# Self-attention's values with transposed probabilities as the weights, queries in the partitions

## The reference

```python
x = x + cross_attention(layernorm(x), ctx_1024)      # softmax(q ctx^T) ctx, one head
x = x + self_attention(layernorm(x), w_attn, w_proj)
x = x + moe_ffn(layernorm(x), Wg, W1, W2, W3)        # 8 experts, each takes its 32 best tokens

def self_attention(x, w_attn, w_proj):               # T = 256, 16 heads of 16
    q, k, v = split(x @ w_attn.T)                    # each (16, T, 16)
    att = einsum('bhqd,bhkd->bhqk', q, k) / sqrt(16)
    att = att + where(rel <= 0, slope[h] * rel, -inf)   # causal, rel = key - query
    y = einsum('bhqk,bhkd->bhqd', softmax(att), v)
    return y.reshape(T, 256) @ w_proj.T
```

## Time and profile before

| | us |
|---|---|
| median of 3 runs | 124.24 |
| lowest and highest | 122.81, 124.9 |
| the profiled execution | 122.81 |
| its span, first to last instruction | 121.1 |
| TensorE busy (matmuls), share | 108.1, 89% |
| VectorE busy, share | 77.5, 64% |
| ScalarE busy, share | 60.3, 50% |

### The profile page before, as it was taken

How to read it: one execution, slowest core, us unless ns; L and a number is a source line. 1 busy time by engine, 2 the same in 40 slices (tenths; PEclk the granted TensorE clock), 3 DMA queues, 4 the chain that set the end, 5 groups by cost and what they waited for, 6 DMA issues and landing times.

```text
span 121.1 us, 2466 instructions
## 1 busy us (share of the span) xinstructions
PE 108.1 (89%) x958; PEld 89.0 (73%) x958; DVE 77.5 (64%) x194; ACT 60.3 (50%) x114; POOL 50.6 (42%) x65
## 2 busy tenths in 40 slices
PE   4999999999999999999998959892987995899981
PEld 4968888888999999999978648681955794334540
DVE  0699889977659697357339799979044797021212
ACT  4377779549869657541248894870011302514100
POOL 2499999999999999911010000010001400300000
PEclk9999999999999999999999999999599999999999
DMA  2995999995999400006989898000000000000002
GB/s 98 375 405 166 401 355 353 419 424 219 346 433 433 179 5 0 0 5 173 520 346 520 346 514 346 11 8 0 5 0 0 0 0 0 5 0 0 0 5 87
DMA packets 3756, 22.72 MB, mean 188 GB/s; under 512 B 544, under 2 KB 800, under 8 KB 3232
## 3 DMA queue, kind: packets, MB, share of 16 engines
q1 hardware_dynamic: 3744, 22.55, 47.1%
HBM read 22.29 MB, written 0.26 MB: 186 GB/s over the span
## 4 chain that ended last, share of the span: by engine, by line
PE 78%; DVE 15%; issue 3%; ACT 1%; POOL 1%; POOLq 0%
PE bank L842 6%; PE bank L844 6%; PE bank L843 6%; PE bank L816 6%; PE bank L820 6%; PE bank L823 6%; PE bank L935 6%; PE bank L1028 6%; PE bank L832 6%; PE bank L798 3%; PE bank L904 3%; PE bank L1043 3%; PE bank L882 3%; DVE att_T L562 3%; PE bank L916 2%
## 5 line engine op out<-in xcount | busy, mean ns | idle before, releaser
L360 POOL TENSOR_TENSOR rstd<-vareps,power 128x1 f32<-128x1 f32 x6 | 3.3, 553 | 41.7 <-DVE vareps L450 41.6
L399 POOL TENSOR_SCALAR bias<-rel 128x384 f32<-128x384 f32 x16 | 20.0, 1254 | 1.1
L842 PE MATMUL bank<-v_hi,p_hi 128*128 128x258 f32 x64 | 19.4, 303 | 0.0
L844 PE MATMUL bank<-v_hi,p_lo 128*128 128x258 f32 x64 | 18.0, 282 | 0.0
L843 PE MATMUL bank<-v_lo,p_hi 128*128 128x256 f32 x64 | 18.0, 281 | 0.0
L498 DVE TENSOR_TENSOR p_lo<-bank,p_hi 128x512 fp32r<-128x512 f32 x16 | 10.9, 686 | 7.9 <-ACT p_hi L680 7.9
L680 ACT ACTIVATE p_hi<-bank 128x512 fp32r<-128x512 f32 x16 | 9.6, 598 | 8.1 <-PE bank L832 8.1
L798 PE MATMUL bank<-ident 128*128 128x128 f32 x74 | 11.5, 319 | 1.7 <-POOL ident L354 1.6
L798 PEld LDWEIGHTS bank<-ident 128*128 128x128 f32 x74 | 10.7, 225 | 2.3 <-POOL ident L354 1.6
L726 ACT ACTIVATE att<-att,nmax 128x128 f32<-128x128 f32 (+1 forms) x32 | 11.9, 444 | 0.8 <-DVE nmax L554 0.8
L843 PEld LDWEIGHTS bank<-v_lo,p_hi 128*128 128x128 f32 x64 | 12.2, 190 | 0.0
(11 more groups left out here) (120 smaller groups left out, 198.6 us busy)
## 6 DMA issues: line engine op xcount, KB each, us to landing
k_in<-ctx_t SPq DMA_DIRECT2D x8, 512.0 KB, 4.6
v_in<-ctx_v SPq DMA_DIRECT2D x8, 512.0 KB, 6.3
wdn_sb<-w_down SPq DMA_DIRECT2D x2, 2048.0 KB, 9.5
wup_hi<-w_up SPq DMA_DIRECT2D x1, 4096.0 KB, 11.9
wup_lo<-w_up SPq DMA_DIRECT2D x1, 4096.0 KB, 18.4
wqkv_sb<-w_qkv SPq DMA_DIRECT2D x1, 768.0 KB, 10.9
x_sb<-x_in SPq DMA_DIRECT2D x1, 256.0 KB, 2.7
wproj_sb<-w_proj SPq DMA_DIRECT2D x1, 256.0 KB, 11.0
```

Source lines behind the costliest of these rows:

```text
L399: nc.gpsimd.tensor_scalar(bias[:, h], rel[:, :], SLOPES[h], None, ALU.mult).then_inc(bias_ready, 1)
L842: nc.tensor.matmul(hi, p_hi[:, h % PB, n], v_hi[:, i, n], start=(i == 0 and n == 0), stop=False)
L844: last = nc.tensor.matmul(hi, p_lo[:, h % PB, n], v_hi[:, i, n], start=False, stop=(i == NCH - 1 and n == NT - 1))
```

## The change

Values are computed the other way round. The transposed probabilities of one head (128 keys by 128 queries) become the weights, and v of the head with a column of ones behind it (17 columns, v_one) streams. So queries lie in the partitions, the sum of the probabilities is the 17th column, and all 16 heads of a block lie side by side in one bank (16 x 17 columns). It is done unit by unit, behind the unit's copy. A block's y is normalized with a reciprocal of 128x16 and one multiply, then transposed by two more transposes on TensorE, copied by ScalarE and projected. Queues are reordered on three engines: q comes before k; VectorE does q of block 1 between units 1 and 2; copy 2 goes to ScalarE, copy 8 to VectorE; values(1) stands behind transpose 2.

```diff
-ACT_COPIES = (3, 5, 7, 8)
+ACT_COPIES = (2, 3, 5, 7)
-        vpad = sb("vpad", [P, TB, 2 * (UW + HD)])
+        v_one = sb("v_one", [P, TB, NH, HD + 1])
-        y_bank = [[banks[4], banks[5]], [banks[5], banks[4]]]
-        proj_ps = [banks[4][:, C:2 * C], banks[3][:, 0:C]]
+        y_ps = [banks[i][:, 0:NH * (HD + 1)].rearrange("p (s d) -> p s d", d=HD + 1) for i in (4, 5)]
+        yT_ps = [banks[i][:, 0:C].rearrange("p (o t) -> p o t", o=NO) for i in (4, 5)]
+        proj_ps = [banks[i][:, C:2 * C] for i in (4, 5)]
...
-            nc.gpsimd.memset(vpad[:, :, :], 0.0).then_inc(vzero_ready, 1)
-            nc.gpsimd.memset(onespad[:, :], 0.0).then_inc(const_step, 1)
-            pool.wait_ge(const_step, 4)
-            nc.gpsimd.memset(onespad[:, HD:2 * HD], 1.0).then_inc(consts_ready, 1)
+            nc.gpsimd.memset(v_one[:, :, :, :], 1.0).then_inc(ones_ready, 1)
...
-            def normalize_y(o, b):
-                cols = slice(b * P, (b + 1) * P)
-                dve.wait_ge(y_in_psum, TB * b + o + 1)
-                step(nc.vector.reciprocal(r_T[:, o, cols], y_bank[b][o][:, P:2 * P]))
-                nc.vector.tensor_tensor(y_T[:, o, cols], y_bank[b][o][:, 0:P], r_T[:, o, cols],
-                                        ALU.mult).then_inc(y_T_ready, 1)
+            def normalize_y(b):
+                dve.wait_ge(y_in_psum, b + 1)
+                step(nc.vector.reciprocal(rsum[:, b], y_ps[b][:, :, HD]))
+                nc.vector.tensor_tensor(y_n[:, b].rearrange("p (s d) -> p s d", d=HD), y_ps[b][:, :, 0:HD],
+                                        rsum[:, b].unsqueeze(2).to_broadcast([P, NH, HD]),
+                                        ALU.mult).then_inc(y_n_ready, 1)
...
-            for n in range(4):
-                bias_unit(n)
-
-            dve.wait_ge(qkv_in_psum, 5)
+            bias_unit(0)
+            bias_unit(1)
+
+            dve.wait_ge(qkv_in_psum, 4)
             dve.wait_ge(qmask_ready, 1)
             nc.vector.tensor_scalar(q_m[:, 0, :, P:2 * P], q_ps[1], qmask[:, 0:1], None, ALU.mult)
             nc.vector.tensor_scalar(q_m[:, 1, :, P:2 * P], q_ps[1], qmask[:, 1:2], None, ALU.mult).then_inc(q_ready[1], 1)
+            bias_unit(2)
+            bias_unit(3)
             copy_transposed(0)
             bias_unit(4)
             copy_transposed(1)
             bias_unit(5)
-            copy_transposed(2)
             bias_unit(6)
             bias_unit(7)
             copy_transposed(4)
-            normalize_y(0, 0)
-            normalize_y(1, 0)
+            normalize_y(0)
             bias_unit(8)
             bias_unit(9)
             copy_transposed(6)
             bias_unit(10)
             bias_unit(11)
             add_projected(0)
+            copy_transposed(8)
             copy_transposed(9)
-            normalize_y(0, 1)
+            norm_apply(2, 0)
             copy_transposed(10)
-            norm_apply(2, 0)
             copy_transposed(11)
-            normalize_y(1, 1)
+            normalize_y(1)
             add_projected(1)
...
+            def copy_y_T(b):
+                scalar.wait_ge(yT_in_psum, b + 1)
+                nc.scalar.activation(y_T[:, :, b * P:(b + 1) * P], yT_ps[b], ACT.Copy).then_inc(y_T_ready, 1)
...
-                for which, ps in ((1, k_ps), (0, q_ps)):
+                for which, ps in ((0, q_ps), (1, k_ps)):
...
-            def values_of_heads(o, b):
...
+            def values_of_unit(n):
+
+                b, heads, keys, r = unit(n)
+                wait_copied(pe, n)
+                pe.wait_ge(v_one_ready, b + 1)
+                for m, (o, u) in enumerate(heads):
+
+                    half, j = divmod(2 * r + u, 4)
+                    column, slot = HPT * half + 4 * o + j, HPT * o + 2 * j + half
+                    for k in range(b + 1):
+                        block = (b + 1) * m + k
+                        last = nc.tensor.matmul(y_ps[b][:, slot], att_T[n // 4][:, r, block * P:(block + 1) * P],
+                                                v_one[:, k, column], start=(k == 0), stop=(k == b))
+                if n in (3, NU - 1):
+                    last.then_inc(y_in_psum, 1)
+
+            def transpose_y(b):
+                pe.wait_ge(y_n_ready, b + 1)
+                for o in range(NO):
+                    last = nc.tensor.transpose(yT_ps[b][:, o], y_n[:, b, o * P:(o + 1) * P], ident[:, :])
+                last.then_inc(yT_in_psum, 1)
...
             transpose_unit(0)
+            scores_round(1)
+            transpose_unit(1)
+            transpose_unit(2)
             values(1)
-            scores_round(1)
-            for n in range(1, 5):
-                transpose_unit(n)
...
+            values_of_unit(0)
+            values_of_unit(1)
+            transpose_unit(3)
+            values_of_unit(2)
+            transpose_unit(4)
+            values_of_unit(3)
+            scores_round(2)
             transpose_unit(5)
-            scores_round(2)
+            values_of_unit(4)
             transpose_unit(6)
+            values_of_unit(5)
+            transpose_y(0)
             transpose_unit(7)
+            values_of_unit(6)
             pe.wait_ge(wproj_loaded, 16)
             project(0)
...
+            for n in range(8, NU):
                 transpose_unit(n)
+                values_of_unit(n - 1)
+            values_of_unit(NU - 1)
             norm_T(2, 0)
+            transpose_y(1)
             project(1)
```

More of the change, by code:

```diff
@@ L103, in build @@
         qmask = sb("qmask", [P, 2])
-        onespad = sb("onespad", [P, 3 * HD])
         slot_no = sb("slot_no", [P, CAP])
@@ L167, in build @@
         y_T = sb("y_T", [P, NO, T])
-        UW = 32 * NH // 2
-        vpad = sb("vpad", [P, TB, 2 * (UW + HD)])
-        v_slots = [vpad[:, b].rearrange("p (u n) -> p u n", u=2)[:, :, 0:UW].rearrange(
-            "p u (m d) -> p u m d", d=32)[:, :, :, 0:HD] for b in range(TB)]
+        v_one = sb("v_one", [P, TB, NH, HD + 1])
         nmax = sb("nmax", [P, NU, 4])
-        r_T = at("r_T", [P, NO, T], split_probs + PB * CH * 4)
+        rsum = sb("rsum", [P, TB, NH])
+        y_n = at("y_n", [P, TB, C], split_probs + PB * CH * 4)
         over_v = [over_v_first]
@@ L207, in build @@
         k_ps, q_ps = ([banks[i][:, 0:C].rearrange("p (m t) -> p m t", m=2) for i in pair] for pair in ((1, 4), (0, 5)))
-        v_ps = [banks[i][:, 0:C] for i in (4, 7)]
+        v_ps = [banks[4][:, 0:C], banks[5][:, C:2 * C]]
         as_bank, at_bank = banks[0:4], banks[6:8]
-        y_bank = [[banks[4], banks[5]], [banks[5], banks[4]]]
-        proj_ps = [banks[4][:, C:2 * C], banks[3][:, 0:C]]
+        y_ps = [banks[i][:, 0:NH * (HD + 1)].rearrange("p (s d) -> p s d", d=HD + 1) for i in (4, 5)]
+        yT_ps = [banks[i][:, 0:C].rearrange("p (o t) -> p o t", o=NO) for i in (4, 5)]
+        proj_ps = [banks[i][:, C:2 * C] for i in (4, 5)]
         router_ps = banks[0][0:E, 0:T]
@@ L263, in build @@
         k_ready = sem("k_ready")
-        vpad_ready = sem("vpad_ready")
+        v_one_ready = sem("v_one_ready")
         rel_step = sem("rel_step")
@@ L267, in build @@
         bias_ready = sem("bias_ready")
-        vzero_ready = sem("vzero_ready")
+        ones_ready = sem("ones_ready")
         ascores_ready = sem("ascores_ready")
@@ L275, in build @@
         y_in_psum = sem("y_in_psum")
+        y_n_ready = sem("y_n_ready")
+        yT_in_psum = sem("yT_in_psum")
         y_T_ready = sem("y_T_ready")
         proj_ready = sem("proj_ready")
-        x_added = sem("x_added")
         router_in_psum = sem("router_in_psum")
@@ L531, in _ @@
             lo_of(*P_TILES[TB * NCH - 3])
-            dve.wait_ge(consts_ready, 4)
+            dve.wait_ge(consts_ready, 3)
             nc.vector.tensor_reduce(qmask[:, :], headmask[:, :].rearrange("p (r u) -> p u r", u=2), AX.X,
@@ L713, in copy_v @@
                 scalar.wait_ge(qkv_in_psum, 3 * b + 3)
-                nc.scalar.activation(v_slots[b], v_ps[b].rearrange("p (u m d) -> p u m d", u=2, d=HD),
-                                     ACT.Copy).then_inc(vpad_ready, 1)
+                nc.scalar.activation(v_one[:, b, :, 0:HD], v_ps[b].rearrange("p (m d) -> p m d", d=HD),
+                                     ACT.Copy).then_inc(v_one_ready, 1)
             def copy_k(b):
-                scalar.wait_ge(qkv_in_psum, 3 * b + 1)
+                scalar.wait_ge(qkv_in_psum, 3 * b + 2)
                 nc.scalar.activation(k_T[:, :, b * P:(b + 1) * P], k_ps[b], ACT.Copy).then_inc(k_ready, 1)
@@ L738, in _ @@
             nc.scalar.activation(q_m[:, 1, :, 0:P], q_ps[0], ACT.Copy, scale=qmask[:, 1:2]).then_inc(q_ready[0], 1)
-            scalar.wait_ge(vzero_ready, 1)
+            copy_k(0)
+            scalar.wait_ge(ones_ready, 1)
             copy_v(0)
@@ L744, in _ @@
             exp_unit(1)
-            copy_v(1)
             exp_unit(2)
             exp_unit(3)
+            copy_transposed(2)
+            copy_v(1)
             exp_unit(4)
@@ L753, in _ @@
             exp_unit(7)
```

(14 more changed lines are left out.)

22 lines of the change are left out of this document (3 added, 19 removed).

## The result

The changed kernel takes 127.57 us (median of 6 runs, 124.7 to 132.2), the kernel before beside it 122.73 (121.88 to 124.9); ratio 1.0239, interval 1.0147 to 1.0331. In later runs it was 126.53 against 122.13, ratio 1.033 (1.0191 to 1.0469). The forecast was 124.4 and no clear change. The changed kernel is slower, since both intervals lie above 1; whether by more than 2% the intervals leave open. What came true is the rival on TensorE's clock.

What follows compares the result with a forecast made beforehand. Self-attention was taken as bound by TensorE from 67.6 us on: 19.7 us of work, 0.4 of stall and the tail put the second addition at 90.7 us, +0.15 on 124.24, so 124.4 us; range 122.0 to 128.5.

Steps and rivals of the forecast that it cites:

- the rival on TensorE's clock: Self-attention, 69 to 87 us: TensorE's clock falls amid weight loads; 1.6 us a spell, 127.7 us with two; chance 0.26.
- The cost of a record: Values on TensorE: each record loading 128 columns and streaming 17 costs 0.112 us; 96 records, 10.75 us.
- the bounds: Values, per record: 0.067 us (faster load, 121.0 us, chance 0.11) or 0.192 us (serial loads, 132 us, chance 0.05).
- TensorE as the bound from 67.6 us on: Self-attention after scores_round(1) starts: TensorE works without a break for 19.69 us, except one stall before unit 8.
- The stall before unit 8: TensorE waits 0.4 us for copy 8, which VectorE does only after the first projection's addition.
- The reciprocal: Normalization on VectorE: a 128x16 reciprocal takes 0.27 us, on the line between 0.17 (128x1) and 0.95 (128x128).
- the tail from normalize to addition: End of self-attention: normalize, transpose, copy and whole projection take 2.8 us, against 2.0 before.
- The front: Start of self-attention: scores start 0.3 us sooner, but scores_round(1) only at 67.6 us against 67.73.
- The sum at full clock: From scores_round(1) at 67.6 us to the second addition at 90.7 us, against 90.61 before.
- the 1.6 us of before's spell: Last values of the kernel before: 64 records take 3.51 us at half clock, 1.88 earlier; this spell leaves the path.
- the clock at 1.0 throughout from 69 to 88 us: Sign on TensorE in self-attention: granted clock 1.0 throughout if the forecast is right; wrong if it reads 0.5 anywhere.
- the second addition within 0.7 us of 90.6: Sign at the end of self-attention: the second projection's addition, forecast at 90.7 us, lies within 0.7 us of 90.6.

Runs made afterwards that it cites:

- a_wideall: The changed kernel with 128 streamed columns instead of 17 in the values of both blocks; 124.22 us, ratio 1.017 to the kernel before.
- a_half64: The changed kernel with 64 streamed columns in all values and block 1's first 128 keys left out (32 of 96 records); 121.36 us, output not the reference's.
- a_r_wideall: The changed kernel with fp32r operands (one record per matmul) and 128 streamed columns in all values; 120.14 us, ratio 0.983 to the kernel before.
- a_wide64: The changed kernel with 64 streamed columns instead of 17 in the values of both blocks; 123.8 us, ratio 1.013 to the kernel before.
- after_again: The changed kernel run once more with no edit; 126.53 us, ratio 1.033 to the kernel before.
- b_warm2: The kernel before plus unread matmuls: eight in TensorE's gap before the last values, two pairs in the router's gaps; 121.49 us, ratio 0.994.

## Why the prediction was right or wrong

**Luck.** The measured 127.57 us lies in the range of 122.0 to 128.5 us, because that range took in two half-clock spells. It is not the mechanism of the forecast that put it there: the changed kernel's median is 4.8 us over that of the kernel before, where the forecast had 0.15. The forecast added its difference to 124.24 us, the median of three runs of the kernel before; the median of six is 122.73.

**The cost of a record** was put at 0.112 us and is 0.111. The choice between the bounds was right too: not 0.067, not 0.192. The rule of the Trainium skill ("TensorE: Matmul & The Clock Gate", "What overlaps and what doesn't") that a load overlaps a running matmul only when row groups differ is not borne out here: loads of one row group stand 0.111 us apart with streams of 17 columns (after) and of 128 (a_wideall) alike, about the 0.109 us that the prediction estimated for the loading alone.

**TensorE as the bound from 67.6 us on** holds: a_half64 and a_r_wideall get faster by what is taken from TensorE's queue (3.6 and 5.3 us), less about 1 us, most of it VectorE's copies (S falls by 2.44 and 4.42). The stall before unit 8 was put at 0.4 us and is 0.50 on the load side, 0.26 on the stream side. The reciprocal was put at 0.27 (the line between its two bounds gives 0.26) and is 0.26 us; the tail from normalize to addition at 2.8 and is 2.85 in a_wide64 (88.14 to 90.99).

**The front** was put at 0.1 us of gain and costs 0.1. The scores start 0.23 us sooner after the first q matmul (2.74 us against 2.97), but the two q_m between units 1 and 2, with their wait of 0.19 us, and the 0.15 us until TensorE takes up the last bias, eat more than that.

**The sum at full clock** was S = 90.7 - 67.6 = 23.1 us. a_wide64 has 23.14 and a_wideall 23.52. Against the earlier trace rows, whose S of 22.88 holds a spell of its own, that is 0.3 to 0.6 us more, where the sum has 0.2. But the 1.6 us of before's spell were counted as a gain, though about a third of its runs have no spell, and no new one was assumed to come.

**The clock** is the step that failed. The trace of before had no row with loads of 128 columns beside short streams; I took the gap-free queue as the argument against a fall, gave the rival 0.26, and priced it at 1.6 us a spell in S. Two of the prediction's own signs failed with it: the clock at 1.0 throughout from 69 to 88 us, and the second addition within 0.7 us of 90.6 (it starts at 93.87). The rival's mechanism was right. The price was near: over a_wide64, S is 25.42 - 23.14 = 2.3 us longer in the first profile, with one spell of 7 us in it, and 26.39 - 23.14 = 3.3 us in after_again with two. (The rival's 127.7 for two spells should read 127.6, 124.4 + 3.2.)

What the rival missed is that the spells can reach beyond S. In the first profile R is 2.4 us longer than before. Lines of TensorE's timeline, before and then after:

```profile
90.41 1.95 PE L798 MATMUL bank<-ident 128*128 128x128 f32 x16
...
93.40 1.15 PE L990 MATMUL bank<-xnT,wg_sb 128*8 128x128 f32 x8
...
103.25 3.64 PE L1028 MATMUL bank<-wup_lo,xg_T 128*32 128x512 f32 x32 [0.64 <-DVE xg_T L641]
```
```profile
93.62 3.61 PE L800 MATMUL bank<-ident 128*128 128x128 f32 x16
...
97.38 1.15 PE L990 MATMUL bank<-xnT,wg_sb 128*8 128x128 f32 x8
...
107.24 5.34 PE L1028 MATMUL bank<-wup_lo,xg_T 128*32 128x512 f32 x32 [0.64 <-DVE xg_T L637]
```

The warming matmuls run at half clock (3.61 us against 1.95), so the router's first matmuls (L990) start 3.51 us after the second addition and not 2.79: 0.7 us. The experts begin in another spell (L1028, 5.34 us against 3.64): 1.7 us. Together with S that is 4.7 of the 5.7 us. This is one profile: in after_again the second spell also reaches the warming matmuls, but ends sooner (95.8 us), they take 2.79 us, and R is 27.44.

The Trainium skill, same page, section "Part 4: PE-mode transpose", says that transposes do not count as matmuls do. By that rule, as the prediction priced it, the clock should have stayed low from 69 to 87 us, about 143 us in all; it did not (1.00 up to 84 us). With wide values between the same transposes it never fell in S, which fits the rule but does not prove it: no run here has transposes alone.

**Against a kernel without spells** the change is dearer than its ratio of 1.013 in a_wide64 says: b_warm2 has S = 21.36, a_wide64 23.14, 1.8 us more (1.5% of 121.49), for an estimated 5.1 us of added loads against 4.2 us of waits and a shorter VectorE queue. These terms were all in the sum, as parts that cancelled only because the profile of before held 1.5 us of half clock.

## What to carry to other kernels

Turning a product round so that the large operand becomes the weights costs its loads, here 0.11 us for 128 columns in each pass, however little streams; count records before counting columns, and with fp32 count twice. Against the kernel before it paid only once the values were single-pass (fp32r), and there the share of the type alone was not measured. A queue full of loads did not hold the clock here. Where a load of 128 columns hides the stream anyway, stream 64 or 128 columns into a place that nobody reads: that held the clock in S, and with 64 columns S came to 23.14 us where the sum for 17 at full clock was 23.1. And before a change is judged by a few per cent, look at how many half-clock spells each profile holds, behind the edited stretch too, and at the mean clock of all runs: the one profile of the kernel before held a spell that about a third of its runs do not have, and the prediction counted its end as a gain.

## What the hardware showed that I had not expected

The granted clock fell to 0.50 while TensorE was busy 3.00 of 3.00 us (84 to 87 us), with 28 streams and 29 loads in it (it stood at 0.98 over these 3 us and at 0.50 from 87 us on), and stayed there to 97 us through further thin values, a projection and warming matmuls, with TensorE idle for about 0.8 us of these ten. With the same loads and streams of 64 or 128 columns it held 1.00 over the whole of S in three profiles. Where the spell comes differs from execution to execution of the same kernel: 87 us in one, 75 and 89 us in the other. In the kernel before, 16 of 51 executions show a mean clock of 0.994 or more and the others 0.986 or less, with nothing changed.
